# Layer norm and gate logits per row tile inside the attention and neighbour loops

## What is computed

```python
x = x + gnn0(ln(x), adj, weight, bias, node_w, edge_w)   # h = ln(x) @ edge_w; softmax over h @ h.T masked by adj
x = x + ffn0(ln(x), Wg, bg, W1, W3, W2)                  # logits = ln(x) @ Wg + bg; top 2 of 8 experts
x = x + gnn1(ln(x), adj, W, b)                           # relu((adj @ ln(x)) @ W.T + b)
x = x + ffn1(ln(x), gate_w, w1, b1, w2, b2)              # logits = ln(x) @ gate_w.T; top 2 of 8 experts
```

## Time and profile before

| | us |
|---|---|
| median of 3 runs | 1930.34 (1928.85 to 1933.15) |
| the profiled execution: time, and its span | 1930.79, 1929.1 |
| attention, steady part | 108 to 642 |
| gate0 with its barriers | 642 to 729 |
| neighbours | 1124 to 1355 |
| gate1 | 1355 to 1440 |
| TensorE busy | 1616.7 (84%) |
| VectorE busy | 998.9 (52%) |

### The profile page before, as it was taken

One profiled execution on the slowest core, in us unless ns is written; L12 is line 12 of the kernel. 1 busy time (PEld: TensorE's weight loads), 2 busy tenths in 40 slices (PEclk: granted clock), 3 DMA queues, 4 the chain that ended last, 5 costly groups with the idle time before them and its releaser, 6 DMA issues. The chain is left out here.

```text
span 1929.1 us, 33709 instructions
## 1 busy us (share of the span) xinstructions
PE 1616.7 (84%) x9896; PEld 1359.9 (70%) x9896; DVE 998.9 (52%) x2483; ACT 663.1 (34%) x1397; POOL 482.4 (25%) x812
## 2 busy tenths in 40 slices
PE   5999999999999737899997069999728999999990
PEld 4888888888888636788776035555617888888880
DVE  5555555555555374655553733232386555566543
ACT  2333332333333202222222523333204455455454
POOL 0111211211120004555454000000014455444530
PEclk9999999999999658999999579999559999999995
DMA  4123334333433551111111833433850111111118
GB/s 152 44 104 149 117 135 152 123 117 143 149 117 99 216 193 39 46 49 49 46 52 49 275 110 121 136 123 113 315 210 30 35 38 37 34 38 33 38 31 286
DMA packets 84840, 209.46 MB, mean 109 GB/s; under 512 B 8896, under 2 KB 66241, under 8 KB 80577
## 3 DMA queue, kind: packets, MB, share of 16 engines
q1 hardware_dynamic: 68192, 154.95, 23.0%
q0 software_dynamic: 11328, 30.95, 5.2%
q10 hardware_dynamic: 5280, 23.09, 3.0%
HBM read 150.89 MB, written 58.07 MB: 108 GB/s over the span
## 5 line engine op out<-in xcount | busy, mean ns | idle before, releaser
L1068 PE MATMUL bank<-ffn_w_in_parts,ffn_x_t 128*128 128x512 f32 x1416 | 362.5, 404 | 18.9 <-DVE ffn_w_in_parts L1195 18.9
L1068 PEld LDWEIGHTS bank<-ffn_w_in_parts,ffn_x_t 128*128 128x128 f32 x1416 | 259.2, 191 | 77.9 <-DVE ffn_w_in_parts L1195 28.3
L1092 PE MATMUL bank<-ffn_w_out_parts,ffn_hidden_t 128*128 128x256 f32 x2124 | 287.1, 290 | 26.5 <-DVE ffn_hidden_t L1184 26.5
L1092 PEld LDWEIGHTS bank<-ffn_w_out_parts,ffn_hidden_t 128*128 128x128 f32 x2124 | 265.5, 193 | 30.9 <-issue 20.0
L508 PE MATMUL bank<-h_t,attn_h_tile 128*128 128x512 f32 (+1 forms) x1092 | 249.1, 383 | 3.8 <-POOL attn_h_tile L389 3.8
L543 PE MATMUL bank<-support,attn_probs_t 128*128 128x512 f32 x650 | 246.4, 412 | 1.1 <-DVE attn_probs_t L424 1.1
L508 PEld LDWEIGHTS bank<-h_t,attn_h_tile 128*128 128x128 f32 x1092 | 196.9, 189 | 46.1 <-issue 4.0
L412 ACT CAST attn_probs_t<-bank 128x512 fp32r<-128x512 f32 (+1 forms) x182 | 98.6, 557 | 349.0 <-PE bank L517 349.0
L1134 ACT ACTIVATE ffn_silu_or_gelu<-bank,w_b_in 128x128 f32<-128x128 f32 x472 | 134.6, 368 | 191.0 <-PE bank L1079 191.0
L424 DVE TENSOR_TENSOR attn_probs_t<-bank,attn_probs_t 128x512 fp32r<-128x512 f32 (+1 forms) x182 | 116.5, 652 | 161.7 <-ACT attn_probs_t L412 161.7
L545 PE MATMUL bank<-support,attn_probs_t 128*128 128x256 f32 x676 | 184.7, 279 | 0.0
(11 more groups left out here) (233 smaller groups left out, 2237.9 us busy)
## 6 DMA issues: line engine op xcount, KB each, us to landing
adj_tile<-in_adj SPq DMA_DIRECT2D x25, 1663.5 KB, 8.4
mask<-attn_mask ACTq DMA_DIRECT2D x26, 832.0 KB, 3.4
nbr_mask<-mask SPq DMA_DIRECT2D x26, 832.0 KB, 4.5
comb_y<-y SPq DMA_DIRECT2D x12, 768.0 KB, 9.9
w_w_in<-in_w SPq DMA_DIRECT2D x2, 4096.0 KB, 16.8
w_w_in<-in_w_t SPq DMA_DIRECT2D x2, 4096.0 KB, 17.5
x_normed<-x SPq DMA_DIRECT2D x6, 768.0 KB, 6.6
xn<-x_normed SPq DMA_DIRECT2D x6, 768.0 KB, 35.5
```

Source lines behind the costliest of these rows:

```text
L1068: ins = pe.matmul(bank[2 + 2 * slot + b][:, :], XT[:, slot, xp, k, :], WIP[:, wp, k, b * CH:(b + 1) * CH], start=n == 0 and k == 0, stop=n ...
L1092: ins = pe.matmul(bank[7][:, 0:D], HTT[:, hp, k, :], WOP[:, wp, k, :], start=n == 0 and k == 0, stop=n == 2 and k == KH - 1)
```

## The change

The layer norm and the logits leave the two gate stages and go into the loops of the stages ahead of them. A new class `Gate` holds the tiles and semaphores. For each row tile DVE aggregates mean and variance behind the row sums; POOL works out the reciprocal deviation in eight operations on 128x1 and one that norms the tile; SP stores the normed tile; and DVE makes each of the eight logits by one multiply-and-sum over 256 columns, of the normed tile with one column of the gate weights. The weights lie broadcast in all partitions as [column in block, block, expert], so that neighbouring columns of one expert are 16 floats apart. In the gate stages the loads of x, the norm, the transposes, the gate matmuls and the stores of `xn` are gone. `w_in` of the second expert stage is loaded by SP in the neighbour stage behind its fourth tile, `w_out` at the start of the gate stage.

```diff
+class Gate:
...
+    def stats(self, dve, t, slot):
+        dve.bn_stats(self.ROW[:, slot, :], self.XO[:, slot, :]).then_inc(self.sums_ready, 1)
+        dve.wait_ge(self.sums_ready, t + 1)
+        if not known(t) or t >= 2:
+            dve.wait_ge(self.normed, t - 1)
+        dve.memset(self.TAKER[:, E:E + 1], 0.0)
+        dve.bn_aggr(self.MV[:, slot, :], self.ROW[:, slot, :]).then_inc(self.stats_ready, 1)
...
+        pool.wait_ge(self.stats_ready, t + 1)
+        link(pool.tensor_tensor(v, var, eps, ALU.add))
+        link(pool.tensor_tensor(minus, mean, minus_one, ALU.mult))
+        link(pool.tensor_tensor(r, v, minus_half, ALU.pow))
...
+        if not known(t) or t >= 2:
+            pool.wait_ge(self.xn_stored[slot], uses * 16)
+            pool.wait_ge(self.summed, (t - 1) * E)
+        pool.tensor_tensor(self.POOL_TAKER[:], eps, eps, ALU.add)
+        pool.tensor_scalar(self.XN[:, slot, :], self.XO[:, slot, :], minus, r, ALU.add, ALU.mult).then_inc(self.normed, 1)
+
+    def store(self, sp, t, slot):
+        sp.wait_ge(self.normed, t + 1)
+        sp.dma_start(self.xn[bass.ds(t * P, P), :], self.XN[:, slot, :]).then_inc(self.xn_stored[slot], 16)
...
+        for e in experts:
+            dve.tensor_tensor_reduce(out=self.PR[:, e], in0=self.XN[:, slot, :].rearrange("p (k q) -> p k q", k=KD),
+                                     in1=self.GW[:, :, :, e].rearrange("p q k -> p k q"), scale=1.0, scalar=0.0,
+                                     op0=ALU.mult, op1=ALU.add, accum_out=self.LS[:, slot, e:e + 1]).then_inc(self.summed, 1)
...
@@ attend, SP @@
                     if not first:
                         store(t - 2, slot)
+                    if not known(t) or t >= 3:
+                        gate.store(sp, t - 3, 1 - slot)
...
```

```diff
...
@@ attend, POOL @@
+                    if not known(t) or t >= 3:
+                        gate.norm(pool, t - 3, uses - 2 + slot, 1 - slot)
                     if not first:
                         pool.wait_ge(adj_in[slot], uses * 16 + (16 if last else 0))
...
@@ attend, DVE @@
-                    rest(t, slot, range(EARLY, NG))
+                    for g in range(EARLY, NG):
+                        rest(t, slot, [g])
+                        if g - EARLY < 4 and not (first and slot == 0):
+                            gate.sums(dve, t - 1, 1 - slot, range((g - EARLY) * 2, (g - EARLY) * 2 + 2))
+                    if not (first and slot == 0):
+                        gate.logits(dve, t - 1, 1 - slot)
...
@@ route, SP @@
-                for sem, (lo, hi) in zip(x_loaded, spans):
-                    sp.dma_start(X[:, lo:hi, :], view[:, lo:hi, :]).then_inc(sem, 16)
-
-                sp.wait_ge(x_loaded[-1], 16)
-                w.load(sp)
...
+                load(sp)
...
@@ neighbours, SP @@
+                    if not known(t) or t >= 3:
+                        gate.store(sp, t - 3, 1 - slot)
                     if not first:
                         store(t - 2, slot)
                     sp.dma_start(XB[:, slot, :], a["x2"][bass.ds(t * P, P), :]).then_inc(x_loaded[slot], 16)
+                    if known(t) and t == 3:
+                        w.load_in(sp)
...
@@ neighbours, DVE @@
                     odd(t, slot, 1, first)
+                    if not known(t) or t >= 3:
+                        logits(t - 3, 1 - slot)
                     odd(t, slot, 3, first)
                     if not very_first:
                         finish(t - 1, uses - (1 - slot), 1 - slot, first)
                     if last:
+                        logits(t - 2, slot)
                         add(t, slot, False)
                         finish(t, uses, slot, False)
+                        logits(t - 1, 1 - slot)
+                        logits(t, slot)
...
```

More of the change, by code:

```diff
@@ L39, with tiles @@
 PAIR_ROWS = 2 * NP
-def tiles(eng, count, step):
+def tiles(eng, count, step, head=2):
     turns = (count - 2) // 2
-    step(0, 0, 0, True, False)
-    step(1, 0, 1, True, False)
-    with eng.Fori(1, turns) as i:
+    for t in range(head):
+        step(t, t // 2, t % 2, t < 2, False)
+    with eng.Fori(head // 2, turns) as i:
         step(i * 2, i, 0, False, False)
@@ L319, in attend @@
         x_out = [s.sem(f"x_stored{i}") for i in range(2)]
-        sums_ready = s.sem("sums_ready")
+        gate = Gate(s, XO, gate_w, gate_b, LG, a["xn"])
         def rows(dram, t):
@@ L358, in step @@
                         sp.dma_start(XB[:, slot, :], rows(a["x"], t)).then_inc(x_in[slot], 16)
-                tiles(sp, T, step)
-                store(T - 2, T % 2)
-                store(T - 1, (T - 1) % 2)
+                tiles(sp, T, step, head=4)
+                gate.store(sp, T - 3, (T - 3) % 2)
+                for t in (T - 2, T - 1):
+                    store(t, t % 2)
+                    gate.store(sp, t, t % 2)
+                gate.end(sp)
                 for slot in range(2):
@@ L394, in _ @@
                 pool.wait_ge(edge, 1)
-                tiles(pool, T, step)
+                gate.constants(pool)
+                tiles(pool, T, step, head=6)
+                for t in range(T - 3, T):
+                    gate.norm(pool, t, t // 2, t % 2)
             @block.scalar
             def _(act):
+                gate.load(act)
                 def step(t, uses, slot, first, last):
@@ L492, in _ @@
                 tiles(dve, T, step)
+                gate.sums(dve, T - 1, (T - 1) % 2, range(E))
+                gate.logits(dve, T - 1, (T - 1) % 2)
             @block.tensor
@@ L688, in route @@
         tile_hot, hot_ready, hot_used = s.sem("tile_one_hot"), s.sem("one_hots_ready"), s.sem("one_hots_used")
-        BLOCKS = [(j, k) for j in range(GROUP) for k in range(KD)]
-        NCONST = 12 if gate_b is None else 11
+        NCONST = 10
         with nc.Block() as block:
@@ L1264, in _, with neighbours @@
                 tiles(dve, S, step)
-def neighbours(nc, a, bank, XH):
+def neighbours(nc, a, bank, XH, gate_w, LG, w):
     GS = [(g, min(8, T - g)) for g in range(0, T, 8)]
@@ L1307, in step @@
                     sp.dma_start(XB[:, slot, :], a["x2"][bass.ds(t * P, P), :]).then_inc(x_loaded[slot], 16)
-                tiles(sp, T, step)
-                store(T - 2, 0)
-                store(T - 1, 1)
+                    if known(t) and t == 3:
+                        w.load_in(sp)
+                tiles(sp, T, step, head=4)
+                gate.store(sp, T - 3, (T - 3) % 2)
+                for t in (T - 2, T - 1):
+                    store(t, t % 2)
+                    gate.store(sp, t, t % 2)
+                gate.end(sp)
                 for slot in range(2):
@@ L1320, in _ @@
                                        pattern=[[-1, P]], channel_multiplier=1).then_inc(consts, 1)
+                gate.constants(pool)
+                tiles(pool, T, lambda t, uses, slot, first, last: gate.norm(pool, t, uses, slot))
             @block.tensor
@@ L1441, in finish, with logits @@
                     dve.wait_ge(x_ready, t + 1)
-                    dve.bn_stats(a["ST"][:, t, :], XO[:, slot, :]).then_inc(sums_ready, 1)
+                    gate.stats(dve, t, slot)
+                def logits(t, slot):
+                    gate.sums(dve, t, slot, range(E))
+                    gate.logits(dve, t, slot)
                 def step(t, uses, slot, first, last):
```

182 lines of the change are left out of this document (90 added, 92 removed).

## The result

The changed kernel takes **1903.5 us** (median of 4 runs, 1901.4 to 1907.2) against 1931.7 us before (4 runs, one more than in the table above, 1928.9 to 1934.5): ratio **0.9861, 95% interval 0.9841 to 0.9880**. It is faster by 1.4%. The prediction said 1960 us, slower, with a chance of 0.42 on faster. The measured time is near the one worked out for the first rival (1902) and inside the range of 1897 to 1978.

What follows compares the result with a forecast made beforehand. The prediction took PE to bound the loops and the gate stages to be chains of their own length. Its terms, -76.4 + 43 + 8 + 19 + 20 + 16 = +29.6 us, gave 1960 us, range 1897 to 1978.

Steps and rivals of the forecast that it cites:

- first rival: Whole kernel: one strided operand costs nothing, multiply-and-sums 0.40 us apart, 1902 us in all, faster; chance 0.36.
- What bounds the kernel: Attention and neighbour loops are bound by PE; the two gate stages are chains whose length is their own.
- What goes: Gate stages: the expert choice starts 39.2 and 37.2 us earlier after the change, -76.4 us.
- tails: Work left behind the loops: +8 us after attention, +16 us for three sets of eight multiply-and-sums in the neighbours.
- What one multiply-and-sum costs: DVE, start to start: 0.40 us at the low end, 0.64 with strided weights; the high end was taken.
- What a pair waits for: Attention tile: the first pair, due at 427.97, stands still until POOL's mask ends at 429.2.
- Attention loop, +43: Late remainders, logit add and aggregation hold PE up 1.8 us a tile, for 24 tiles +43 us.
- The sign that the prediction named: Attention loop: PE idle in front of the products with `support`, 1.5 us a tile.
- Neighbours, the weights, +19: Neighbour tile 4: its mask queues behind `w_in`, PE stands 17.5 us, plus 1.5 for a lowered clock.
- Neighbours, the loop, +20: Sums and POOL waits, 6.6 us, overrun 5.7 us of room between `odd` operations; 0.6 to 0.9 us for 22 tiles.
- The sum: Whole kernel: all terms together give +29.6 us on the profiled 1930.8, 1960 us, slower; chance 0.50.
- The second rival: Whole kernel: slow multiply-and-sums but no standstill at POOL's mask, 1930 us, no change; chance 0.14.

Runs made afterwards that it cites:

- e4: Changed kernel plus a stage timing single DVE operations on 128x256, alone and beside POOL; strides from 16 bytes added 0.16 to 0.19 us.
- e8: Changed kernel plus a stage timing DVE operations on 128x208, alone and beside POOL's mask; 370 ns packed, 506 at 64 bytes, 540 at 104.
- e1: Changed kernel with the gate weights laid out packed, without gaps between columns; ratio 0.9806.
- e11: Changed kernel with a third, unused multiply-and-sum of 80 columns in each pair, making a pair 1.28 us; ratio 0.9955.
- e2: Changed kernel with the second layer's `w_in` loaded in its gate stage again, not in the neighbour loop; ratio 0.9754.
- e9: Changed kernel with a third, unused multiply-and-sum of 192 columns in each pair, making a pair 1.48 us; ratio 1.0154.
- e3: Changed kernel with the attention pairs of multiply-and-sums placed one remainder later; ratio 0.9828.

## Why the prediction was wrong, point by point

- **What bounds the kernel: right.** PE bounds the loops, and DVE's 120 us more work in attention (405.1 us in 534, for 285.1 in the earlier trace rows) costs 9.9.
- **What goes: right.** The prediction's 76.4 us less its tails (8, and 10.7 for the two sets of sums behind the last tile) is 57.7; the two stretches to the expert choice lost 61.9. With the tails apart: attention 11.2 - (44.3 - 39.2) = 6.1 us for +8; neighbours 12.9 - (41.7 - 37.2) = 8.4, and 9.6 for 3.9 us in the last tile, 5.7, in all 14.1 for +16.
- **What one multiply-and-sum costs: the first step that failed.** "I take the high end", 0.64 us; it is 0.52. The direction of the argument held: SBUF operands with gaps cost, and one strided operand costs as much as two (e4). L839 was PSUM and no guide to it: a copy from PSUM takes 368 ns packed and 369 at 32 bytes (e8). The size came from L872, whose access costs 0.92 ns a column, where 64 bytes cost 0.65 (e8). Besides, the low end of 0.40 was too high: packed it is 0.35 (e1, e4). So the bounds were 0.12 and 0.05 too high. The truth lay above the 0.50 at which, by the prediction, the first rival decides, and the change was clearly faster all the same, so the price alone cannot be what turned the sign.
- **What a pair waits for: right in kind, too late in place.** The standstill at POOL's mask is there, in the tile shown above and by itself in e4. The prediction put the mask's end 1.23 us after the first pair is due (429.2 less 427.97). In the tile shown it is 0.81 (413.91 less 413.10). The new DMAs on SP's queue were charged with 0.94 us (426.2 less 425.26); the mask starts 1.53 us ahead of the remainder instead of 2.02 as in the earlier trace rows, so 0.49; over 18 middle masks it is 1.49 instead of 2.08, so 0.6.
- **Attention loop, +43: +9.9.** The second step that failed. At the prediction's own price it is 548.7 - 522.2 = +26.5 (e11), 1.09 us a middle tile and not 1.8; 4.2 of the 26.5 us lie in the one tile beside the last mask. Of the 0.7 us a tile, 0.6 is there by the second remainder, 2.50 us behind the first for 3.12. The rest, with the 0.3 us charged for the logit add and the aggregation, was not tried by itself. From +26.5 to +9.9 it is the price. The sign that the prediction named, 1.5 us of idle in front of the products with `support` in each tile, did not appear (5.4 us in the whole loop). A slip in its sum changes nothing: 408.93 + 21.10 is 430.03, not 430.05.
- **Neighbours, the weights, +19: 19.4.** Right in place, cause and size: the wait of 17.5 us was 17.64, the granted clock had fallen to 0.50 in it, and 1.8 us for the 1.5 charged were lost behind it. The terms that are written down (1153.2, 21.4 and 2) give 1176.6, not 1177.5; the 0.9 us that are not explained match what passed in the changed kernel between the issue of the small load (1131.73) and of the second `w_in` (about 1132.7). e2 takes the wait away, and 19.4 us with it.
- **Neighbours, the loop, +20: nothing.** The third step that failed, and not by the price. A middle tile is 8.63 us before, after and in e11. The 5.7 us of room was right: the time from the end of the first `odd` to the start of the second is 4.5 us in the changed kernel and 5.5 in e11, which fit, and 6.3 in e9, where a tile is 0.7 us longer. Wrong were the 1.3 us for waits on POOL's small operations, which would have made it 6.6 at the price of e11. DVE hardly waits; POOL does (below).
- **The sum.** e11 is 0.9955 x 1930 = 1921 us: with its price granted, the forecast would have been 39 us too high. The price moves 1921 to 1903, 18 us. So two thirds of the error of 57 us lie in turning DVE's work into time (16.5 us in the attention loop and 20 in the neighbours' of the 39) and one third in the operation. The sign, too, was lost there: with 39 us less the forecast would have been faster even at 0.64 us. The first rival's 1902 came out by chance: its price of 0.40 us was not the price of this kernel, its +12 and +1 for the loops were near +9.9 and 0, and its +9.5 for the neighbours' tail was 14.1. With sums as cheap as that rival had them, or a little cheaper, the attention loop is 3.6 us longer and not 12 (e1: 525.8 - 522.2), so its way from price to time was too dear as well.
- **The second rival**, slow sums without a standstill, is not what happened: the standstill is there, and moving the pairs away from it is worth 6.4 us (e3).
- **"Wrong would be the forecast if the record is 0.42":** the record is 0.60, and it was wrong all the same, by its conversion.

## What to carry to other kernels

Before a DVE operation with gaps between its columns is put into a tuned loop, lay the constant operand out packed: it is free on the host, and here it was worth 10.6 us of 1903. When a price is borrowed from another row, compare the stride in bytes too, not only the number of strided operands. Added work on an engine with slack is cheap until a period is full and then costs at every repetition (here 0.4, 1.1 and 2.0 us a tile for 1.04, 1.28 and 1.48 us a pair); so work out the period, and where two engines hold each other up, find out which of them really stands before charging the wait. A weight load belongs where the chain is long and the queue otherwise empty, not ahead of a load that PE needs.

## What the runs showed of the hardware that was not expected

- DVE's price by stride, fp32 in SBUF, two sources: nothing at 8 bytes, 0.63 to 0.75 ns a column at 16, 32 and 64 bytes (e4, e8), 0.8 to 0.9 at 104 (e8); from PSUM nothing at 8 bytes (434 ns both ways, e4); a copy with one source at 64 bytes 384 ns for 280 packed (e4).
- DVE's standstill beside POOL's long operation is not limited to two SBUF operands: a copy and a `tensor_scalar` of fp32 with one SBUF source took 3.03 us too (e8); a memset (e8), and a sum with one operand in PSUM (e4), did not stand.
- Where DVE runs two-operand sums back to back, it keeps its pace in the neighbours' loop (0.51 us each) and POOL is the one that is slowed; in e4 two of eight sums beside POOL's norm were slowed too. In the neighbours POOL's norm and its small operations take more than twice their time in attention, where DVE then works on PSUM operands:

```profile
L211 POOL TENSOR_SCALAR attn_x_normed<-attn_x_out,attn_rstd x26: 553/555/557, 124.9 to 657.0; 128x256 f32<-128x256 f32 x26
...
L211 POOL TENSOR_SCALAR nbr_x_normed<-nbr_x_out,nbr_rstd x26: 552/1344/1782, 1126.2 to 1364.1; 128x256 f32<-128x256 f32 x26
...
L204 POOL TENSOR_TENSOR nbr_rstd<-nbr_rstd,nbr_constants x26: 189/435/442, 1125.2 to 1362.6; 128x1 f32<-128x1 f32 x26
```
